# Step order of a fused attention, expert and filter kernel: first sends on two queues, modulation in group 3, second tile's weights before the attention's end, mode products shifted

## What is computed

```python
x = x + L0(x)   # attention: 16 heads of 16, softmax(q k^T / 4) under a mask, out-projection, RMS norm,
                # then * rms_scale * (1 + sc) + shift, where [shift, sc] = silu(cond) @ Wc.T + bc
x = x + L1(x)   # gate: top 2 of 8 experts per token; each expert is relu(relu(x W1 + b1) W2 + b2) W3 + b3
x = x + L2(x)   # ((x @ input_basis.T) * cond_256) @ (orthogonalised mode_to_rank) * cond_64 @ output_basis
x = x + L3(x)   # quaternion rotation of the channels, one gate value per channel
```

## Time and profile before

| | us |
|---|---|
| median of 3 runs (lowest, highest) | 1217.4 (1215.42, 1218.43) |
| the profiled execution, own time | 1216.96 |
| its span | 1215.2 |
| PE busy / DVE / ACT / POOL in the span | 1139.1 / 824.7 / 736.8 / 534.0 |
| first layer1 of the experts on PE | 663.9 |
| last layer3 ends | 1165.1 |

### The profile page before, as it was taken

The page is one execution under the profiler, slowest core; times in us unless marked ns, Lnnn a source line. Parts: engine busy times, 40 slices in busy tenths (PEclk is TensorE's granted clock), DMA queues, the critical chain, the costliest instruction groups (busy, mean ns, idle before and its releaser), DMA issues.

```text
span 1215.2 us, 23411 instructions
## 1 busy us (share of the span) xinstructions
PE 1139.1 (94%) x7533; PEld 769.8 (63%) x7590; DVE 824.7 (68%) x2331; ACT 736.8 (61%) x1632; POOL 534.0 (44%) x805
## 2 busy tenths in 40 slices
PE   6899999999989989998888899999999999999978
PEld 3333433434434334343322899999999999999968
DVE  4688879687897887877772444464555655667647
ACT  2266666575666666666546566566666666666645
POOL 7234225484673765747535347546222222323210
PEclk9899999999999999999889899999999999999999
DMA  6654635647448455483543658975655774833536
GB/s 194 185 192 153 200 114 178 200 166 196 136 162 258 140 165 159 153 251 104 177 173 118 228 152 283 340 220 114 189 152 133 233 233 121 277 61 67 157 87 208
DMA packets 101456, 213.52 MB, mean 176 GB/s; under 512 B 10885, under 2 KB 71181, under 8 KB 92886
## 3 DMA queue, kind: packets, MB, share of 16 engines
q1 hardware_dynamic: 87030, 193.34, 49.3%
q0 software_dynamic: 14304, 18.69, 8.3%
HBM read 239.15 MB, written 74.29 MB: 258 GB/s over the span
## 4 chain that ended last, share of the span: by engine, by line
PE 67%; POOL 11%; issue 5%; DVE 5%; DMA 4%; ACT 3%; SPq 3%; another core or an unknown queue 0%; DVEq 0%; POOLq 0%; ACTq 0%
PE bank L1023 36%; PE bank L1123 6%; PE bank L1092 5%; PE bank L1104 5%; PE bank L1108 4%; POOL routed L1882 3%; DMA w_parts<-in_W 2%; PE bank L1068 2%; PE bank L1141 2%; DVE junk L1551 1%; ACT pt L1284 1%; POOL ssq L793 1%; SPq L879 1%; PE bank L1181 1%; PE bank L1076 1%
## 5 line engine op out<-in xcount | busy, mean ns | idle before, releaser
L1284 ACT ACTIVATE pt<-bank 128x512 f32<-128x512 f32 x512 | 300.5, 595 | 178.2 <-PE bank L1108 125.2
L1551 DVE CUSTOM_DVE_ANT_0 junk<-bank,mneg 128x512 bf16<-128x512 f32 x512 | 336.1, 684 | 100.5 <-PE bank L1092 99.5
L1023 PE MATMUL bank<-hid,w 128*128 128x256 f32 x1872 | 241.9, 286 | 4.2 <-DVE hid L1699 4.2
L1699 DVE TENSOR_TENSOR hid<-full,hid 128x256 fp32r<-128x256 f32 x312 | 138.4, 449 | 148.0 <-ACT full L1358 145.8
L1892 POOL DMA_INDIRECT x<-yout,rows x78 | 122.6, 1572 | 263.8 <-ACT yout L1363 235.5
L1023 PEld LDWEIGHTS bank<-hid,w 128*128 128x128 f32 x1872 | 228.6, 191 | 5.2 <-issue 3.1
L1353 ACT ACTIVATE hid<-bank,biases 128x256 fp32r<-128x256 f32 x312 | 150.7, 483 | 103.5 <-PE bank L1023 102.7
L1358 ACT ACTIVATE full<-bank,biases 128x256 f32<-128x256 f32 x312 | 150.3, 482 | 0.0
L1108 PE MATMUL bank<-mneg,identb 128*128 128x512 bf16 x391 | 149.9, 383 | 0.0
L1023 PE MATMUL bank<-rowsT,w 128*128 128x256 f32 x936 | 122.8, 285 | 6.1 <-DMA w<-split_weights 5.2
L1123 PE MATMUL bank<-pt,vaug 128*17 128x512 f32 x1024 | 124.3, 604 | 1.9 <-ACT pt L1284 0.7
(11 more groups left out here) (184 smaller groups left out, 1492.3 us busy)
## 6 DMA issues: line engine op xcount, KB each, us to landing
w<-split_weights SPq DMA_DIRECT2D x80, 1024.0 KB
w<-split_weights SPq DMA_DIRECT2D x40, 2048.0 KB
split_weights<-w_parts SPq DMA_DIRECT2D x64, 512.0 KB, 4.2
w_parts<-in_W SPq DMA_DIRECT2D x64, 256.0 KB, 4.5
split_parts<-parts SPq DMA_DIRECT2D x28, 384.0 KB, 2.6
rows<-routed SPq DMA_DIRECT2D x39, 258.0 KB, 3.6
stacks<-split_parts SPq DMA_DIRECT2D x36, 256.0 KB, 7.4
qst<-split_parts SPq DMA_DIRECT2D x24, 256.0 KB, 7.6
```

Of the source, the lines that this page charges most:

```text
L1023: product = T.matmul(ps, w[p], x[q], start=(k == 0 and n == 0), stop=(k == len(weights) - 1 and n == 2))
L1284: A.activation(pt[n % len(pt)][:, :], bank[3 + n % 2][:, :], ACT.Exp, scale=float(D) ** -0.5).then_inc(exped.sem, 1)
L1551: V.tensor_tensor_reduce(junk[n % 2][:, :], bank[n % 3][:, :], mneg[:, 0, st, :], 1.0, FLOOR, ALU.add, ALU.max, rowmax[gi % 2][:, hh, st:s ...
L1699: V.tensor_tensor(lo, h[:, :], hi.bitcast(F32), ALU.subtract).then_inc(hidden_low.sem, 1)
```

## The change

Cut to its core; `...` marks what is left out.

```diff
+FIRST_SENDS = ((0, 2, 4), (1, 3), (5,)), ((1,), (), (4,))
+FIRST_KEY_SENDS = ((0, 0),), ((5, 0), (2, 1), (3, 1))
...
-TABLE_PARTS = 4
+TABLE_PARTS = 5
...
 chain(b):
     out.append(("residual", b))
-    for _ in range(9 if b == KNOWN else 6):
+    for _ in range(13 if b == KNOWN else 6):
         yield
...
     out.append(("count", b))
-    for _ in range(6):
+    for _ in range(5 if b == KNOWN - 1 else 6):
         yield
     out.append(("place", b))
...
             out.append(("scatter", b, k, st))
-            if st % 2:
+            if st % 2 or b < KNOWN - 1:
                 yield
...
 attention_order:
             step = ("project", 0, qk, half)
-            out.extend((step, ("rest",) + step[1:], ("part",) + step[1:]))
-        for qk, part in ((0, 0), (0, 1), (1, 0), (0, 2), (1, 1), (1, 2)):
+            if (qk, half) == (1, 0):
+                out.append(("masks", 0))
+            out.extend((step, ("rest",) + step[1:]))
+            if qk:
+                out.append(("send_key", half, 0))
+            out.append(("part",) + step[1:])
+        out.append(("send_key", half, 1))
+        for qk, part in ((0, 0), (0, 1), (1, 0), (0, 2), (1, 2)):
             out.append(("send", qk, half, part))
-        if half == 0:
-            out.append(("masks",))
-    out.append(("constants",))
+    out.extend((("masks", 1), ("constants",)))
...
-        if i == 0:
+        if i == 3:
             todo += [("prepare",), ("modulation",)]
...
+            if (i, k) == (GROUPS + 1, 3):
+                out.append(("stacks",))
+                for layer in range(3):
+                    out.append(("fetch_weights", layer, 1))
...
 expert_order:
-    out.append(("experts", "transfers"))
+    out.extend((("experts", "transfers"), ("fetch_biases", 1)))
     fetch_rows(2)
-    out.append(("fetch_biases", 1))
-    for layer in range(3):
-        fetch(layer, 1)
...
-    assert next(side, out) is out and next(later, out) is out
-    for b in range(2, B, 2):
-        for step in ("ranked", "mixed", "combined"):
-            out.extend(((step, b), (step, b + 1)))
+    assert next(later, out) is out
+    for _ in side:
+        pass
+    for b in range(2, B + 2):
+        for step, behind in (("ranked", 0), ("combined", 2), ("mixed", 0)):
+            if 2 <= b - behind < B:
+                out.append((step, b - behind))
...
+    def stacks_over(queue):
+        queue.wait_ge(*last_col(B - 1))
+        queue.wait_ge(*max_found.at((LAST_GROUP, GH - 1, ST - 1)))
+        queue.wait_ge(*max_turned.at((LAST_GROUP,)))
+        queue.wait_ge(*cleared.at((LAST_GROUP, 2, 0)))
...
 SyncE, loads at the start:
-        start(wv ...)
-        start(mask8[:, 0] ...); start(mask8[:, 1] ...)
-        load_x(1)
+        start(mask8[:, 0] ...)
+        load_x(1)
+        start(wv ...)
+        start(mask8[:, 1] ...)
...
 ScalarE:
+            elif name == "send_key":
+                half, n = at
+                for r, part in FIRST_KEY_SENDS[n]:
+                    act.wait_ge(*(high, middle)[part].at((0, 1, half)))
+                    nc.scalar.dma_start(*first_rows(1, half, part, r)).then_inc(dma_first[half], 16)
...
 VectorE:
                 if b >= 2:
-                    dve.wait_ge(*side_pe.at(("combined", b - 2)))
+                    dve.wait_ge(*side_pe.at(("mixed", b - 2)))
...
-            elif name == "masks":
+            elif step == ("masks", 0):
+                dve.wait_ge(dma_masks[0], 16)
+                V.tensor_scalar(mneg[:, 0], mask8[:, 0], MASKED, None, ALU.mult).then_inc(masks_made, 1)
+            elif step == ("masks", 1):
                 dve.wait_ge(ident_made, 2)
                 V.tensor_copy(identb[:, :], ident[:, :]).then_inc(masks_made, 1)
                 V.memset(bank[5][:, :], 0.0).then_inc(masks_made, 1)
-                dve.wait_ge(dma_masks, 32)
-                V.tensor_scalar(mneg[:, 0], mask8[:, 0], MASKED, None, ALU.mult).then_inc(masks_made, 1)
+                dve.wait_ge(dma_masks[1], 16)
                 V.tensor_scalar(mneg[:, 1], mask8[:, 1], MASKED, None, ALU.mult).then_inc(masks_made, 1)
...
 row: dve.wait_ge(masks_made, 4) becomes dve.wait_ge(masks_made, 1)
 table: part 0 (11 operations) becomes part 0 (4) and part 1 (7); parts 1 to 3 become 2 to 4
```

More of the change, by code:

```diff
@@ L640, in _build @@
     prepared = sem("prepared")
-    TABLE = 3 + 7 + 1, 3, 4, 6
-    tables = Count(sem("tables"), [(s, TABLE[s[2]] + ((0, 0, 0, 5), (2, 0, 0, 0))[s[1]][s[2]]) for s in order if s[0] == "table"])
+    TABLE = 4, 7, 3, 4, 6
+    tables = Count(sem("tables"), [(s, TABLE[s[2]] + ((0, 0, 0, 0, 5), (1, 1, 0, 0, 0))[s[1]][s[2]]) for s in order if s[0] == "table"])
     MATRIX = {"gram": 2, "eliminate": 3, "norm": 3, "unit": 1,
@@ L678, in _build @@
     dma_w = [sem(f"dma_weights{i}") for i in range(2)]
-    dma_wv, dma_masks = sem("dma_value_weights"), sem("dma_masks")
+    dma_wv, dma_masks = sem("dma_value_weights"), [sem(f"dma_masks{i}") for i in range(2)]
     dma_cond, dma_wo, dma_small, dma_pad = sem("dma_cond"), sem("dma_wo"), sem("dma_small"), sem("dma_pad")
@@ L702, in _build @@
     CONSTANTS = 23
+    MASKS = 4
     CHANGED = 2 * NTILES
@@ L770, in stacks_loaded, with first_rows @@
                 queue.wait_ge(dma_stack[qk], 16 * len(PAIRS) * b)
+    def first_rows(qk, half, part, r):
+        assert PAIRS[r][qk] == part
+        return ((qst, kst)[qk][0][r:KQ:len(PAIRS), half * (H // 2):(half + 1) * (H // 2), :], parts[qk][:, half, part, :])
     def last_col(b):
@@ L862, in sync_program @@
                 sp.wait_ge(*(high, middle, lows)[part].at((0, qk, half)))
-                for r, pair in enumerate(PAIRS):
-                    if pair[qk] == part:
-                        start((qst, kst)[qk][0][r:KQ:len(PAIRS), half * (H // 2):(half + 1) * (H // 2), :],
-                              parts[qk][:, half, part, :]).then_inc(dma_first[half], 16)
+                for r in FIRST_SENDS[qk][part]:
+                    start(*first_rows(qk, half, part, r)).then_inc(dma_first[half], 16)
             elif name == "part" and at[0]:
@@ L955, in sync_program @@
                 projections_over(sp)
+            elif name == "stacks":
+                stacks_over(sp)
             elif step == ("experts", "transfers"):
@@ L1129, in tensor_program @@
                 pe.wait_ge(*max_split.at((gi,)))
[L1130 removed]
+                pe.wait_ge(masks_made, MASKS)
                 pe.wait_ge(constants_made, CONSTANTS)
@@ L1545, in vector_program @@
                 dve.wait_ge(*row_scored.at((gi, hh, st)))
-                dve.wait_ge(masks_made, 4)
+                dve.wait_ge(masks_made, 1)
                 if n >= 2:
@@ L1648, in vector_program @@
                     v(V.tensor_copy, tb[:, 1], tb[:, 0])
+                elif part == 1:
                     for i, width in enumerate((1, 2, 4)):
@@ L1654, in vector_program @@
                         v(V.tensor_tensor, shifted, base, taken, ALU.subtract)
-                elif part == 1:
+                elif part == 2:
                     v(V.tensor_tensor, tj[:, 0, 0:n], over_tiles(end, n), over_experts(number, n), ALU.is_le)
@@ L1658, in vector_program @@
                     v(V.tensor_scalar, left8, expert, -1.0, float(NX), ALU.mult, ALU.add)
-                elif part == 2:
+                elif part == 3:
                     v(V.tensor_tensor, tj[:, 1, 0:n], over_tiles(rev, n), over_experts(left8, n), ALU.is_equal)
@@ L1663, in vector_program @@
                     v(V.tensor_tensor, chunk, number, first_tile, ALU.subtract)
-                elif part == 3:
+                elif part == 4:
                     if not late:
```

13 lines of the change are left out of this document (6 added, 7 removed).

## The result

The changed kernel takes 1233.9 us (median of 4 runs, 1233.2 to 1235.1) against 1216.9 of the kernel before beside it: ratio 1.0141, 95% interval 1.0123 to 1.0158. It is 17 us slower where I forecast 14 us faster. The profiled execution has a span of 1231.6 us.

The account below looks back on a forecast made before the run. It took PE work to bound most of the span, with gains only where PE stands still. Terms 4.2 + 4.0 + 4.0 + 0 + 2.0 = 14.2 us off 1216.96 gave 1202.8, 1203 as a median; range 1195 to 1211.

Parts of the forecast that it names:

- stays clear of the late POOL: Chain of batch 6: its root, with 13 pieces instead of 9, avoids the late POOL; counted without cost or gain.
- the slow one: Rival at the handover: PE, SP and POOL form one ring whose delays add 19 us, giving 1222; chance 0.07.
- First sends: At the start: SP keeps 16 sends of 24, ACT takes eight, last keys come earlier; 4.2 us gained, bounds 0 and 5.2.
- Modulation: Early attention, moved to turn 3: PE and DVE waits and the low clock behind go; 4.0 us gained, bounds 1.5 and 5.
- Scatters: Seam of chains 4 and 5: spread scatters cut DVE's wait for POOL from 5.28 to 2.1 us; 4.0 gained, bounds 3 and 7.
- Table and handover: Between attention and experts: old waits go, new ones come at rows 0 and biases; 0 us, bounds -4 and +6.
- the handover costs: Rival: rows 0 come later than computed and PE waits at a low clock; some 5 us, 1208; chance 0.11.
- Mode products: Around the last tile: `combined` products 1.77 us apart in the new order; 2.0 us gained, bounds 1 and 3.

Follow-up runs that it names:

- b_shift8_2: Kernel before with 17 pieces instead of 9 for batch 6, so chains of batches 6 and 7 come 8 small steps later; 1233.6 us, ratio 1.0105 on B.
- a_res5_3: Changed kernel with 5 pieces instead of 13 for batch 6, third run; 1220.0 us against 1218.0 of the kernel before, ratio 1.0022.
- b_mod: Kernel before with only the modulation's steps moved behind those of turn 3 instead of turn 0; 1223.4 us in one run, against 1219.8.
- b_spread: Kernel before with scattered stores of batches 0 to 4 one to a small step and 5 pieces for batch 6; 1221.5 us against 1217.4, ratio 1.0036.
- b_same: Kernel before, unchanged, run on chip B for a trace; 1219.0 us.
- best1: Changed kernel with 5 pieces for batch 6 and batch 1's value and stack steps after the first row maxima; 1227.2 us against 1240.9, ratio 0.9886.

## Why the prediction was wrong

**The step that failed** is the sentence that the root of batch 6 with 13 pieces "stays clear of the late POOL", in the list of what moves without cost or gain. I looked at the one place where the root is used and not at what stands behind it. The small steps carry on through the whole chain of batch 7, whose logits stand 145 us behind that root, past a queue that I had not read at all: POOL's adds. Only four of the eight steps come from the 13 pieces; the other four, from the spread scatters, the table's fifth part and `place`, I didn't follow past the handover either. Price: 14 us (`b_shift8_2` adds 14, `a_res5_3` is rid of 15). None of my rivals had this mechanism; the slow one, 0.07, sat at the handover. The trace before showed what was needed: POOL already waits for adds to land (5.69 us at 773.33, 1.89 us at 800.56), and DVE waits for POOL in every chain, being one case.

**First sends**, 4.2 counted, 1.7 measured. The cost of a send on ACT was right. The term failed where I kept 1.85 us from the last issue to the landing: it was read with issue as the limit and held no longer once issue was faster (4.69 us).

**Modulation**, 4.0 counted, 3.4 lost (`b_mod`). The waits that I saw went, but so did SP's, which had kept the order right. I asked what PE and DVE do without the modulation and not what SP does, though its store of the modulation was moved too. The bounds of 1.5 to 5 left out a loss, and gave no reason for that.

**Scatters**, 4.0 counted, 3.1 measured at the seam, with DVE's wait 2.52 us where 2.1 was computed. Right but for the clock, and only together with the edits at the table (`b_spread`).

**Table and handover**, 0 counted, about 4 lost. The mechanism was as foreseen: a gain of 5.7 us on PE between the first exponentials of groups 29 and 30, the wait for rows 0 (5.84 us, computed 4.9), none for the weights, one behind the biases. From group 30 to tile 0 the distance to the kernel before goes from -3.2 to +1.4 in the pair shown, and from -2.3 to +1.8 in `a_res5_3` against `b_same`. That is the rival "the handover costs", which I gave 0.11; the size of my term was off, at its bound of -4. The chain of batch 6, late by its share, adds 3 us more up to tile 3 (`b_shift8_2`: 41.4 us from tile 0 to tile 3, against 38.1), given back by tile 7.

**Mode products**, 2.0 counted, 1.0 measured from tile 34 on (0.7 to 1.8 in the other traces of that code from B, D and E against `b_same`). The pace is 1.91 us instead of 1.77, and the chain that ended last now goes over the landing of a store, 6.94 us.

The sum that I should have had: 1.7 - 3.4 + 3.1 - 4.1 + 1.0 = -1.7, so 1.7 us slower, near the 2.0 us that `a_res5_3` shows, and 14 more for the place of the chains. That this comes so near is partly luck: the terms are differences of single traces, and the start alone differs by up to 5 us among traces of the same code.

## What to carry to other kernels

A piece inserted into a chain moves all that follows it in every queue: before calling it free, list the steps behind it that two engines exchange, and look for waiting instructions (here adds that wait for their predecessors to land) at the places where they will now stand. A wait that is taken away may have been keeping another queue in order, so look at what that queue does with the freed time. A change of a few us is worth timing on more than one chip.

## What the runs showed of the hardware

The same kernel takes 1217 to 1220 us with the result and on chips B, D and E, and 1238 to 1241 us on A and C. On these two, tile 10 to 11 takes 20.4 to 20.7 us instead of 10.9 where eight scattered stores go out in pairs with the chains in their old place, and the granted clock is 0.57 in the 8 us from the middle of the standstill on (`best1`, 836 to 844 us). Kernels are ranked otherwise there: `a_res5` has the ratio 0.9963 and 0.9950 on the two, 1.0022 elsewhere.

A scattered add takes, by the packets of the trace, 3.4 to 3.7 us from the issue of a tile's second add to the last packet in tiles 0, 1, 11 and 12 of the changed kernel, and 8.9, 9.3 and 10.5 us in tiles 5, 6 and 7, where weights load beside it.
